# Expert results weighted per slot and added to the residual in memory by accumulating scatters; bias transposes moved behind the list matmuls

## What is computed

```python
logits = jnp.einsum('bsd,de->bse', input, Wg)            # 8 experts
probs = jax.nn.softmax(logits, axis=-1)
top_vals, top_idx = jax.lax.top_k(probs, 2)
top_vals = top_vals / jnp.sum(top_vals, axis=-1, keepdims=True)
...
h = jax.nn.relu(jnp.einsum('ebsd,edh->ebsh', xm, W1) + b1[:, None, None, :])   # 256 -> 512
y = jnp.einsum('ebsh,ehd->ebsd', h, W2) + b2[:, None, None, :]                 # 512 -> 256
out = jnp.sum(y * jnp.moveaxis(scores, -1, 0)[..., None], axis=0)
...
x = _layernorm(x + out, axis=-1)
```

## Time and profile before

| | us |
|---|---|
| median of 3 runs | 2051.44 (2048.76 to 2051.68) |
| the profiled execution | 2053.94 |
| its span | 2052.2 |
| busy in the span: PE | 1746.8 (85%) |
| busy: DVE | 1191.0 (58%) |
| busy: ACT | 832.0 (41%) |
| busy: POOL | 1323.0 (64%) |

### The profile page before, as it was taken

One profiled execution on the slowest core, in us unless ns is written; L12 is line 12 of the kernel. 1 busy time (PEld: TensorE's weight loads), 2 busy tenths in 40 slices (PEclk: granted clock), 3 DMA queues, 4 the chain that ended last, 5 costly groups with the idle time before them and its releaser, 6 DMA issues. The chain is left out here.

```text
span 2052.2 us, 32755 instructions
## 1 busy us (share of the span) xinstructions
PE 1746.8 (85%) x10682; PEld 1212.3 (59%) x10682; DVE 1191.0 (58%) x2046; ACT 832.0 (41%) x1228; POOL 1323.0 (64%) x711
## 2 busy tenths in 40 slices
PE   7553599999989999998999999899999998509990
PEld 5443466666656666665666666566666664408980
DVE  4788555556565656556565665655565654553345
ACT  3111234444444444444444444444444444224440
POOL 2988338577676667576776676675766677454544
PEclk8775689999999999999999999999999999559995
DMA  5000200000200000010000001000000000321223
GB/s 185 1 21 24 79 1 22 1 22 0 73 1 22 22 3 22 0 52 22 21 1 23 1 21 52 21 22 1 21 1 21 15 1 1 124 84 63 71 63 128
DMA packets 37813, 68.09 MB, mean 33 GB/s; under 512 B 3560, under 2 KB 27504, under 8 KB 36656
## 3 DMA queue, kind: packets, MB, share of 16 engines
q1 hardware_dynamic: 33936, 56.12, 8.1%
q0 software_dynamic: 3744, 10.23, 1.5%
HBM read 52.84 MB, written 13.50 MB: 32 GB/s over the span
## 5 line engine op out<-in xcount | busy, mean ns | idle before, releaser
L1001 POOL TENSOR_TENSOR xa_total<-xa_total,xa_pexp 128x1024 f32<-128x1024 f32 (+1 forms) x352 | 852.9, 2423 | 52.7 <-ACT xa_pexp L942 27.3
L1060 DVE TENSOR_REDUCE xa_parts<-ps_ring 128x1 f32<-128x402 f32 x1024 | 532.3, 565 | 299.8 <-PE ps_ring L887 292.8
L942 ACT ACTIVATE xa_pexp<-ps_s 128x1024 f32<-128x1024 f32 (+1 forms) x416 | 422.7, 1025 | 419.0 <-PE ps_s L842 391.9
L856 PE MATMUL ps_pv<-xa_pexp,xa_v 128*64 128x512 f32 (+1 forms) x1664 | 399.8, 604 | 0.0
L887 PE MATMUL ps_ring<-xa_k_hi,xa_q_hi 64*128 64x402 f32 x1024 | 235.0, 377 | 32.7 <-DVE xa_parts L1060 31.4
L856 PEld LDWEIGHTS ps_pv<-xa_pexp,xa_v 128*64 128x64 f32 (+1 forms) x1664 | 106.2, 137 | 181.9 <-issue 148.3
L887 PEld LDWEIGHTS ps_ring<-xa_k_hi,xa_q_hi 64*128 64x128 f32 x1024 | 142.7, 186 | 118.2 <-DVE xa_parts L1060 58.9
L1001 POOL TENSOR_TENSOR xa_total<-xa_pexp 128x1024 f32<-128x1024 f32 x32 | 76.3, 2384 | 190.9 <-ACT xa_pexp L942 189.6
L1048 DVE TENSOR_TENSOR xa_k_lo<-ps_ring,xa_k_hi 128x402 fp32r<-128x402 f32 (+1 forms) x128 | 73.6, 575 | 214.7 <-ACT xa_k_hi L953 214.7
L842 PE MATMUL ps_s<-xa_q_hi,xa_k_hi 64*128 64x512 f32 (+1 forms) x832 | 194.0, 433 | 3.6 <-DVE xa_k_lo L1048 2.8
L842 PE MATMUL ps_s<-xa_q_neg,xa_row_one 64*128 64x512 f32 (+1 forms) x832 | 174.4, 393 | 0.0
(11 more groups left out here) (263 smaller groups left out, 2946.2 us busy)
## 6 DMA issues: line engine op xcount, KB each, us to landing
wa_raw<-in_pack_a SPq DMA_DIRECT2D x17, 768.0 KB, 4.4
ex_w_raw<-in_pack_e SPq DMA_DIRECT2D x8, 1026.0 KB, 5.3
ctx_raw<-in_ctxT SPq DMA_DIRECT2D x4, 1601.0 KB, 8.5
wb_raw<-in_pack_b SPq DMA_DIRECT2D x16, 256.0 KB, 2.6
ex_w_hi<-ybuf SPq DMA_DIRECT2D x8, 512.0 KB, 7.6
sa_xT<-in_xT SPq DMA_DIRECT2D x8, 256.0 KB, 6.4
X<-in_x SPq DMA_DIRECT2D x1, 2048.0 KB, 11.5
x_hi<-sa_x1s_hi SPq DMA_DIRECT2D x16, 128.0 KB, 2.1
```

The lines of the kernel that those rows point to most:

```text
L856: ins = nc.tensor.matmul(ps_pv[half(h), :], v[0:m, t, at:at + XD], pexp[0:m, buf, h, :], start=t == 0, stop=t == MT - 1)
L942: nc.scalar.activation(pexp[0:m, buf], ps_s[0:m, (p * MT + t) % 2], ACT.Exp, scale=XD ** -0.5)\
L1001: nc.gpsimd.tensor_tensor(total[p][0:m], first, pexp[0:m, buf], ALU.add).then_inc(s["add_done"], 1)
L1060: nc.vector.tensor_reduce(parts[:, h, q, c:c + 1], ps_ring[:, r, 0:CW], AX.X, ALU.max)\
```

## The change

- ybuf goes. In its place stands `acc`, a copy of x2: SP stores every batch of X to both. Both get 128 further rows, which are set to zero at the start from a zeroed part of `xT_f` (new semaphore `zero_out`; ACT waits for it ahead of its first pack, POOL ahead of the gathers). A padding slot p of any block now has row 2048 + p, for gather and scatter alike, so one index table `rows` serves both.
- The weight of each assignment is brought into slot order as the token number is: `norm` is split in three BF16 parts (`part`), each multiplied with the one-hot tensor (three DVE products, behind the list), 32 more matmuls of 117 columns on PE, and one reduction to `weight`.
- DVE's copy of a block's result becomes a multiplication by the slot's weight. The scatter becomes an indirect DMA that adds to acc. Scatter q waits until scatter q-1 has landed (semaphore `added`), since a token has a row in two blocks.
- At the end acc is loaded back to X, 512 KB per batch, and statistics follow at once; the products and additions of L1275, L1590 and L1592 go.
- The transposes of b1 move behind the 32 table matmuls, and ACT takes packs 2, 3, 4 and 5 after gate tiles 3, 7, 11 and 15.

```diff
-    x2 = nc.dram_tensor("x2", [B * N, E], F32, kind="Internal").ap()
-    ybuf = nc.dram_tensor("ybuf", [YROWS, E], F32, kind="Internal").ap()
+    x2 = nc.dram_tensor("x2", [ROWS, E], F32, kind="Internal").ap()
+    acc = nc.dram_tensor("acc", [ROWS, E], F32, kind="Internal").ap()
...
+            sp.wait_ge(s["zero_set"], 1)
+            for dst in (x2, acc):
+                sp.dma_start(dst[B * N:ROWS], xT_f[:, 0].rearrange("p k n -> p (k n)")).then_inc(s["zero_out"], 16)
             for b in range(B):
                 sp.wait_ge(s["x_done"], NC * (b + 1))
-                sp.dma_start(x2.rearrange("(t p) e -> p t e", p=P)[:, tiles(b), :], X[:, tiles(b), :])\
-                    .then_inc(s["x2_out"], 16)
+                for dst in (x2, acc):
+                    sp.dma_start(dst.rearrange("(t p) e -> p t e", p=P)[:, tiles(b), :], X[:, tiles(b), :])\
+                        .then_inc(s["x2_out"], 16)
...
-            for r in range(3):
-                sp.wait_ge(s_out[r], 16 * ((NBK - r + 2) // 3))
+            sp.wait_ge(s["added"], 16 * NBK)
             for b in range(B):
-                for j in range(TOPK):
-                    src = ybuf[j * B * N + b * N:j * B * N + (b + 1) * N].rearrange("(t p) e -> p t e", p=P)
-                    sp.dma_start(back[:, j * T + NC * b:j * T + NC * (b + 1), :], src).then_inc(back_in[b], 16)
+                sp.dma_start(X[:, tiles(b), :], acc.rearrange("(t p) e -> p t e", p=P)[:, tiles(b), :])\
+                    .then_inc(back_in[b], 16)
...
             def scatter(q):
                 pool.wait_ge(s["y_copied"], q + 1)
-                nc.gpsimd.indirect_dma_start(ybuf, bass.IndirectOffsetOnAxis(ap=sidx[:, q:q + 1], axis=0),
-                                             y_sb[:, q % 3, :], None).then_inc(s_out[q % 3], 16)
-
-            pool.wait_ge(s["x2_out"], 16 * B)
+                need(pool, s["added"], 16 * q)
+                nc.gpsimd.indirect_dma_start(acc, bass.IndirectOffsetOnAxis(ap=rows[:, q:q + 1], axis=0),
+                                             y_sb[:, q % 3, :], None, compute_op=ALU.add).then_inc(s["added"], 16)
+
+            pool.wait_ge(s["x2_out"], 2 * 16 * B)
+            pool.wait_ge(s["zero_out"], 32)
...
-                pool.wait_ge(back_in[b], 16 * TOPK)
-                for t in range(NC * b, NC * (b + 1)):
-                    nc.gpsimd.tensor_scalar(back[:, t], back[:, t], norm[:, t, 0:1], None, ALU.mult)\
-                        .then_inc(s["first_added"], 1)
...
             gate(T - 1)
-            pe.wait_ge(s["w_hi_done"], NE)
-            for c in range(HC):
-                ins = nc.tensor.transpose(ps_y[0:NE, 1, c * P:(c + 1) * P], b1c[:, :, c], ident[:])
-            ins.then_inc(s["b1_tr"], 1)
-
...
             ins.then_inc(s["table_mm"], 1)
+            pe.wait_ge(s["w_hi_done"], NE)
+            for c in range(HC):
+                ins = nc.tensor.transpose(ps_y[0:NE, 1, c * P:(c + 1) * P], b1c[:, :, c], ident[:])
+            ins.then_inc(s["b1_tr"], 1)
+            pe.wait_ge(s["wgt_done"], 3)
+            for n in range(ASG):
+                ins = nc.tensor.matmul(ps_h[:, 0, 0:3 * NBK], one_r[:, n], val_q[:, n].rearrange("p a q -> p (a q)"),
+                                       start=n == 0, stop=n == ASG - 1)
+            ins.then_inc(s["wgt_mm"], 1)
...
                 need(pe, s["h_copied"], q - 1)
+                if q == 0:
+                    pe.wait_ge(s["weight_ready"], 1)
...
             nc.scalar.copy(bx[:], zero[:, 0:1].broadcast_to([P, HID + E]))
+            act.wait_ge(s["zero_out"], 32)
             act.wait_ge(s["const_in"], 32)
...
                 nc.scalar.copy(xT_f[:, t % 2].rearrange("p k n -> p (k n)"), ps_x[:, t % 2, 0:E]).then_inc(s["xT_done"], 1)
+                if t % NC == NC - 1:
+                    take_weights(2 + t // NC)
...
-            for e in range(2, NE):
+            for e in range(2 + B, NE):
                 take_weights(e)
...
-            nc.vector.memset(zero[:], 0.0).then_inc(s["zero_set"], 1)
+            nc.vector.memset(zero[:], 0.0)
+            nc.vector.memset(xT_f[:, 0], 0.0).then_inc(s["zero_set"], 1)
...
-            nc.vector.tensor_tensor(norm[:], top[:, :, 0:TOPK], gred[:].unsqueeze(2).broadcast_to([P, T, TOPK]), ALU.mult)
+            link(nc.vector.tensor_tensor(norm[:], top[:, :, 0:TOPK].rearrange("p t j -> p j t"),
+                                         gred[:].unsqueeze(1).broadcast_to([P, TOPK, T]), ALU.mult))
+            flat_norm = norm[:].rearrange("p j t -> p (j t)")
+            for n in range(3):
+                link(nc.vector.tensor_copy(part[:, n], flat_norm))
+                if n < 2:
+                    link(nc.vector.tensor_tensor(flat_norm, flat_norm, part[:, n], ALU.subtract))
...
+            nc.vector.tensor_tensor(rows[:], pad[:], wrap[:], ALU.add).then_inc(s["list_ready"], 1)
+            for n in range(3):
+                nc.vector.tensor_tensor(val_q[:, :, n], one_q[:], part[:, n].unsqueeze(2).broadcast_to([P, ASG, NBK]),
+                                        ALU.mult).then_inc(s["wgt_done"], 1)
...
+            dve.wait_ge(s["wgt_mm"], 1)
+            nc.vector.tensor_reduce(weight[:], ps_h[:, 0, 0:3 * NBK].rearrange("p (a q) -> p q a", a=3), AX.X, ALU.add)\
+                .then_inc(s["weight_ready"], 1)
...
                 if q >= 3:
-                    dve.wait_ge(s_out[q % 3], 16 * (q // 3))
-                nc.vector.tensor_copy(y_sb[:, q % 3], ps_y[:, q % 2, 0:E]).then_inc(s["y_copied"], 1)
+                    dve.wait_ge(s["added"], 16 * (q - 2))
+                nc.vector.tensor_scalar(y_sb[:, q % 3], ps_y[:, q % 2, 0:E], weight[:, q:q + 1], None, ALU.mult)\
+                    .then_inc(s["y_copied"], 1)
...
-                for t in range(NC * b, NC * (b + 1)):
-                    dve.wait_ge(s["first_added"], t + 1)
-                    link(nc.vector.scalar_tensor_tensor(out=X[:, t], in0=back[:, T + t], scalar=norm[:, t, 1:2], in1=X[:, t],
-                                                        op0=ALU.mult, op1=ALU.add))
-                    ins = nc.vector.tensor_tensor(X[:, t], X[:, t], back[:, t], ALU.add)
-                link(ins)
+                dve.wait_ge(back_in[b], 16)
                 statistics(NC * b, s["fvar"])
```

More of the change, by code:

```diff
@@ L1108 @@
 NBK = B * N * TOPK // P + NE - 1
-YROWS = TOPK * B * N + NBK * P
+ROWS = B * N + P
 def experts(nc, a, X, consts, out):
@@ L1140, in experts @@
         idxf = sb("idxf", [P, T, 8])
-        norm = sb("norm", [P, T, TOPK])
+        norm = sb("norm", [P, TOPK, T])
+        part = sb("part", [P, 3, ASG], BF16)
         hot = sb("hot", [P, TOPK, T, NE])
@@ L1161, in experts @@
         row_of, second = sb("row_of", [P, 1]), sb("second", [P, 1])
-        spare = sb("spare", [P, NBK])
+        spare = sb("spare", [P, 1])
         full, wrap, pad = sb("full", [P, NBK]), sb("wrap", [P, NBK]), sb("pad", [P, NBK])
-        gidx, sidx = sb("gidx", [P, NBK], U32), sb("sidx", [P, NBK], U32)
+        rows = sb("rows", [P, NBK], U32)
+        weight = sb("weight", [P, NBK])
         past = sb("past", [P, NBK, NE])
@@ L1177, in experts @@
         h_f, y_sb = sb("h_f", [P, 2, HID]), sb("y_sb", [P, 3, E])
-        back = w_hi[:, 0:4, :].bitcast(F32).rearrange("p a (b e) -> p (a b) e", e=E)
         ps_x = ctx.enter_context(nc.psum_tensor("ps_x", [P, 2, 512], F32))
@@ L1187, in experts @@
                           "digits_ready one_q_done one_r_done val_done table_mm list_ready step "
-                          "g_in0 g_in1 g_in2 s_out0 s_out1 s_out2 xb_tr xb_hi_done xb_done sel_done "
-                          "h_mm h_copied h_tr h_hi_done h_done y_mm y_copied back_in0 back_in1 back_in2 back_in3 first_added "
+                          "g_in0 g_in1 g_in2 added wgt_done wgt_mm weight_ready zero_out xb_tr xb_hi_done xb_done sel_done "
+                          "h_mm h_copied h_tr h_hi_done h_done y_mm y_copied back_in0 back_in1 back_in2 back_in3 "
                           "fvar frstd_half frstd fdone stored")
@@ L1230, in _ @@
             nc.gpsimd.iota(col[:], pattern=[[0, 1]], base=1, channel_multiplier=1, allow_small_or_imprecise_dtypes=True)
-            nc.gpsimd.iota(spare[:], pattern=[[P, NBK]], base=TOPK * B * N + 1, channel_multiplier=1,
-                           allow_small_or_imprecise_dtypes=True)
+            nc.gpsimd.iota(spare[:], pattern=[[0, 1]], base=B * N + 1, channel_multiplier=1, allow_small_or_imprecise_dtypes=True)
             nc.gpsimd.iota(steps16[:], pattern=[[0, NE], [P, T]], base=0, channel_multiplier=0,
@@ L1253, in gather @@
                 nc.gpsimd.indirect_dma_start(xg[:, q % 3, :], None, x2,
-                                             bass.IndirectOffsetOnAxis(ap=gidx[:, q:q + 1], axis=0))\
+                                             bass.IndirectOffsetOnAxis(ap=rows[:, q:q + 1], axis=0))\
                     .then_inc(g_in[q % 3], 16)
@@ L1319, in _ @@
                         pe.wait_ge(s["val_done"], 2)
```

(18 more changed lines are left out.)

5 lines of the change are left out of this document (3 added, 2 removed).

## The result

The changed kernel takes 2062.79 us (median of 6 runs, 2061.01 to 2067.25) against 2051.53 (6 runs, 2048.76 to 2057.37) for the kernel before beside it: ratio 1.0055, 95% interval 1.0039 to 1.0071. It is slower, by 0.55%; 2031.5 was predicted. Its profiled execution took 2063.38 us, span 2061.6.

The account below looks back on a forecast made before the run. Of the last 290 us, PE was taken to bound the block loop, between list-making and a DVE/POOL tail. Terms: -24.0 + 1.0 + 0.2 + 3.7 - 0.8 = -19.9 us, from median 2051.44 to 2031.5 us; range 2026 to 2050.

Parts of the forecast that it names:

- The adding scatter in the loop: Block loop: each scatter waits for the one before; landing taken as 3.4 us, hidden up to 3.7, cost nothing.
- The sign of being wrong that the prediction named: Block loop: a period over 3.85 us would make the forecast wrong; scatters were expected still 3.8 us apart.
- Rival 1: Block loop: the adding scatter paces it, landing up to 4.82 us, +24.1 us, 2075.5 us; chance 0.14.
- The last landing in the tail: Tail: the last adding scatter lands later than a plain one, +1.0 us (0 to +2.1).
- The tail: After the last scatter: multiplications, multiply-adds and additions go, one load per batch, last normalisation 24.0 us sooner.
- The list: Head: routing list ready at 1844.0, +0.2 us (-3.3 to +3), behind the last w_lo subtraction.
- Rival 3: Head: all 16 normalisations finish before w_lo(0), weights 2 and list come 3 us sooner, 2028 us; chance 0.14.
- the landing of weights 2: Head: weights 2 land near 1792.4, behind the last stores of x2: 2.8 us of data, 0.6 to land.
- The wait is moved ahead of the gate, not removed: Head: with early packs ACT waits for weights inside the gate, which ends at 1810.5 instead of 1793.5.
- That last subtraction is what rules the list: Head: POOL's last w_lo, ending 1827.4 against 1828.42, holds back DVE's scan; list 15.4 us after it.
- Weights per slot: Between list and turn_x(0): DVE products 4.4 us and 32 matmuls 3.3 us ahead of the first block, +3.7 us.
- The clock of the first block: First block: PE, busy 3.3 us right before it, may find the clock up from 1.2 GHz, -0.8 us (0 to -1).

Follow-up runs that it names:

- swapped waits: Changed kernel with POOL's two waits before a scatter reversed, landing of the scatter before first, result second: 2039.60 us, timed again 2041.45 us, ratio 0.9946.
- own_rows_add: Changed kernel, each block adding to its own rows of a longer acc, scatters waiting only for their result buffer, sum per token left out: 2028.86 us.
- own_zero: Changed kernel with the zero rows stored from a tile of their own, so ScalarE does not wait until they are stored: 2065.68 us.
- moved_early: Kernel before with only the head reordered: bias transposes behind the list matmuls, packs 2 to 5 taken after gate tiles 3, 7, 11, 15: 2054.85 us.
- y_ahead: Changed kernel with POOL's wait for the weighted result moved ahead of the gather in front of the scatter: 2045.18 us, ratio 0.9965.

## Why the prediction was wrong

- **The adding scatter in the loop: this step failed.** The prediction had "with 0.1 us to wake, anything up to 3.7 us is hidden behind PE's block" and 3.4 us for a landing, and put the cost at nothing. The landing was inside its bounds (2.41 to 4.47) but 3.8 at the median, and over 5 at times; the wake, from landing to next start, was not 0.1 us but 0.77. So the ring is 4.57 us where 3.5 was taken: 0.67 of the excess is the wake, 0.4 the landing. Period 4.70 for 3.81: +33.8 us on the term that stood at 0. The wake alone, with a landing of 3.4, would have made the ring longer than PE's block; and with the short wake of the swapped waits the period is still 4.09, some 11 us lost. The wake was a guess without a row, and no row of the kernel before shows 0.1 us; of all the terms it was the one to bound, since 38 blocks multiply it. The sign of being wrong that the prediction named, a period over 3.85, came.
- Rival 1 named the right ring and POOL's wait in it, with 4.82 us for a landing and 2075.5 in all; it put the turning point at a landing of 4.2 us. As measured that point lies at 3.4: the mean period is the median landing plus 0.9 us (4.70 - 3.8), where the rival had plus 0.1. Its chance of 0.14 was worked out on the landing alone.
- The rule that the prediction cites against the change, from the Trainium skill (Collectives: The Full Stack, "The bandwidth ceiling"), halves the rate where an addition needs two source reads; the page has it for the rings of collectives. It names the right danger and too high a price here: a landing of 3.8 against 2.41 us is 1.6 times, and own_rows_add shows it as harmless until the next scatter waits for it.
- **The last landing in the tail**: +1.0 predicted, +1.3 measured (3.73 against 2.41).
- **The tail**: -24.0 for the time from the landing to the last normalisation, measured 40.9 - 16.4 = -24.5. First load to last normalisation is 12.5 us for 13 predicted. Right, and right in its parts: the load of 512 KB took 3.97 us for 3.95.
- **The list**: +0.2 predicted, -0.3 measured (79.6 for 79.9). The number is right by luck, as two misses cancel. Rival 3's event came: the normalisation slipped ahead of the first subtractions (5.22 us for 13.62), since the zeros landed only at 1770.05 (1761.85 and 8.2 to land). own_zero is close to the head that the forecast described, normalisations and subtractions across each other, and there the list is at 85.5 us: +5.6 for the predicted +0.2. The term that was too small is the landing of weights 2, 3.4 us behind the stores in the prediction: in own_zero they are issued at 1783.86 and ScalarE takes them at 1792.25, 8.4 us later. The slip was worth 5.9 us instead of rival 3's 3, and paid for this. ScalarE's wait between the gate's tiles 3 and 4, in the changed kernel and in own_zero:

```profile
1786.47 0.19 ACT L1395 COPY ex_b1c<-ex_w_raw 128x4 f32<-128x4 f32 x1 [9.07 <-DMA ex_w_raw<-in_pack_e]
...
1792.25 0.19 ACT L1395 COPY ex_b1c<-ex_w_raw 128x4 f32<-128x4 f32 x1 [18.00 <-DMA ex_w_raw<-in_pack_e]
```

  "The wait is moved ahead of the gate, not removed" was right: ScalarE stands 9.07 us there, and moved_early shows the move and the early packs nearly to cancel. "That last subtraction is what rules the list" held as well, at an earlier operation than the scan: in the changed kernel DVE's value at L1498 is stretched to 4.41 us and ends at 1821.61, with POOL's last subtraction (1816.95 + 4.62 = 1821.57).
- **Weights per slot**: +3.7 predicted, measured 7.3 - 4.1 = +3.2. The chain shows the two terms, 4.4 and 3.3 predicted:

```profile
1839.29 4.12 DVE ex_val_q L1564 x3
1843.41 0.05 issue
1843.45 3.33 PE ps_h L1324 x32
```

- **The clock of the first block**: -0.8 predicted, nothing measured: from turn_x(0) to the first scatter are 11.0 us after and 10.9 before. In spite of 3.3 us of matmuls right ahead of it, the granted clock stays at 0.50, the 1.2 GHz level, up to 1852, and is 0.61 in the microsecond behind it; in the kernel before it is 0.50 up to 1852 and 0.61 behind it too. The first block in the trace after still has 1.21 us for two matmuls that take 0.73 in the second:

```profile
1848.28 1.21 PE L1346 MATMUL ps_h<-ex_w_hi,ex_xb_hi 128*128 x2 [1.06 <-DVE ex_xb_lo L1581]
...
1853.13 0.73 PE L1346 MATMUL ps_h<-ex_w_hi,ex_xb_hi 128*128 x2
```

## What to carry to other kernels

When a change makes each step of a loop wait for the step before, lay out the ring: landing, wake, whatever else the engine does between, and compare its sum with the loop's period, with every part bounded from both sides; a term multiplied by the number of blocks deserves the first row. If the ring is the longer by a little, split it (here two accumulators by parity: from +0.55% to -0.6%) before anything else. And ahead of an indirect DMA on GpSimd write the wait that will stall first, so that the DMA instruction itself carries it, and the one that will long be met behind it.

## What the runs showed of the hardware that was not expected

- A wait already met, ahead of a stalling one on GpSimd between two indirect DMAs, delays the next scatter by 0.5 us after the landing (0.77 against 0.27); five kernels agree, and y_ahead has both in one execution. In the traces the wait for the landing is then in an instruction of its own and not on the DMA; what takes the half microsecond is open.
- An indirect scatter that adds holds GpSimd 1.59 us where the plain one holds it 0.99, and lands in 3.8 us (3.6 to 5.7 over all runs) where the plain one took 2.41.
- Taking a wait away made the list 5.9 us later (own_zero), since it let two engines meet that shut each other out.
- Two stores of 128 KB, issued by SP behind 2 MB of loads, took 7.9 and 8.2 us to land.
